# Softmax of the self-attention: two exponentials over 512 columns a slot, and row sums on VectorE

## What is computed

```python
tohd = lambda t: t.reshape(B, N, h, d).transpose(0, 2, 1, 3)
q, k, v = (make_fxp(tohd(q)), make_fxp(tohd(k)), make_fxp(tohd(v)))
dots = make_fxp(jnp.einsum('bhnd,bhmd->bhnm', q, k) * scale)
attn = make_fxp(jax.nn.softmax(dots, axis=-1))
attn = make_fxp(attn)
out = make_fxp(jnp.einsum('bhnm,bhmd->bhnd', attn, v))
```

## Time and profile before

| | us |
|---|---|
| median of 3 runs (lowest to highest) | 730.09 (729.47 to 730.7) |
| span of the profiled execution | 730.2 |
| TensorE matmul busy | 672.8 (92%) |
| VectorE busy | 550.0 (75%) |
| ScalarE busy | 413.7 (57%) |
| GpSimd busy | 272.6 (37%) |
| ScalarE, exponentials of self-attention (L819), x256 | 75.1 |
| ScalarE, their accumulator reads (L819), x256 | 49.9 |
| VectorE, reciprocals of self-attention (L1047), x32 | 6.5 |

### The profile page before, as it was taken

One profiled execution on the slowest core, in us unless ns is written; L12 is line 12 of the kernel. 1 busy time (PEld: TensorE's weight loads), 2 busy tenths in 40 slices (PEclk: granted clock), 3 DMA queues, 4 the chain that ended last, 5 costly groups with the idle time before them and its releaser, 6 DMA issues.

```text
span 730.2 us, 15676 instructions
## 1 busy us (share of the span) xinstructions
PE 672.8 (92%) x5186; PEld 551.7 (76%) x5186; DVE 550.0 (75%) x1142; ACT 413.7 (57%) x1443; POOL 272.6 (37%) x610
## 2 busy tenths in 40 slices
PE   5998879989998899878989999999999889999997
PEld 4777768777886788766777877787788777888986
DVE  5879887887888789757767776677667668787775
ACT  4677756767776777764455455445544563433432
POOL 1166754454445534535354344234333532010110
PEclk9999999999999999999999999999999999999999
DMA  9135100000000000050000000000000000000000
GB/s 312 49 111 150 60 30 1 1 1 1 0 0 0 0 0 0 0 153 1 1 2 16 1 1 1 14 0 0 0 0 0 0 1 1 2 30 0 29 29 29
DMA packets 17002, 18.75 MB, mean 26 GB/s; under 512 B 2851, under 2 KB 15427, under 8 KB 16963
## 3 DMA queue, kind: packets, MB, share of 16 engines
q1 hardware_dynamic: 15330, 15.11, 6.4%
q0 software_dynamic: 1632, 3.15, 1.5%
HBM read 16.16 MB, written 2.10 MB: 25 GB/s over the span
## 4 chain that ended last, share of the span: by engine, by line
PE 35%; POOL 7%; DVE 6%; ACT 3%; issue 3%; DVEq 0%; POOLq 0%; ACTq 0%
PE bank L405 9%; PE bank L407 8%; PE bank L406 8%; POOL p_f L363 6%; PE bank L583 3%; ACT e_sb L889 2%; PE bank L595 2%; PE bank L607 1%; DVE mx L1164 1%; PE bank L729 1%; PE bank L741 1%; DVE bn_st L966 1%; DVE oT_lo L1206 1%; POOL p_int L316 0%; DVE v_sb L1137 0%
## 5 line engine op out<-in xcount | busy, mean ns | idle before, releaser
L363 POOL TENSOR_SCALAR p_f<-e_sb,rsum 128x128 f32<-128x128 f32 x256 | 95.6, 398 | 156.7 <-DVE rsum L1199 156.7
L316 POOL TENSOR_SCALAR p_int<-e_sb,rsc 128x128 int16<-128x128 f32 x256 | 116.2, 475 | 6.3 <-issue 5.7
L889 ACT ACTIVATE e_sb<-bank,neg_max 128x128 f32<-128x128 f32 x256 | 90.1, 380 | 12.1 <-DVE neg_max L1168 11.9
L804 ACT ACTIVATE sgn<-bank 128x512 bf16<-128x512 f32 x96 | 57.2, 598 | 57.6 <-PE bank L407 57.6
L819 ACT ACTIVATE e_sb<-si 128x128 f32<-128x128 int16 x256 | 75.1, 303 | 0.0
L1021 DVE SCALAR_TENSOR_TENSOR ri<-sgn,bank 128x512 int16<-128x512 bf16 x96 | 62.5, 677 | 7.3 <-ACT sgn L804 6.5
L875 ACT COPY q_sb<-bank 128x512 f32<-128x512 f32 x32 | 18.8, 587 | 84.5 <-PE bank L407 84.5
L311 POOL TENSOR_TENSOR rsc<-rsum,growth 128x8 f32<-128x8 f32 x32 | 6.7, 209 | 156.0 <-DVE rsum L1047 156.0
L889 ACT ACTIVATION_READ_ACCUMULATOR e_sb<-bank,neg_max 128x1 f32 x256 | 55.9, 218 | 0.0
L405 PE MATMUL bank<-xnT_hi,wqkvT_lo 128*128 128x512 f32 x128 | 53.6, 419 | 2.2 <-DVE ri L1021 1.3
L1175 DVE COPY aT_sb<-bank 128x512 f32<-128x512 f32 x64 | 41.2, 685 | 12.7 <-PE bank L583 12.5
(11 more groups left out here) (162 smaller groups left out, 2039.5 us busy)
## 6 DMA issues: line engine op xcount, KB each, us to landing
x_sb<-in_x SPq DMA_DIRECT2D x4, 512.0 KB, 10.3
wqkv_raw<-in_L_attn_w_qkv SPq DMA_DIRECT2D x2, 1024.0 KB, 10.2
out<-x_sb SPq DMA_DIRECT2D x8, 256.0 KB, 2.2
wqkv_raw<-in_L_attn_w_qkv SPq DMA_DIRECT2D x2, 512.0 KB, 5.1
wp_raw<-in_L_attn_w_proj SPq DMA_DIRECT2D x1, 1024.0 KB, 12.3
raw_b<-in_L_xattn_Wq SPq DMA_DIRECT2D x2, 512.0 KB, 3.3
wq_hi<-in_L_xattn_Wq POOLq DMA_DIRECT2D x2, 512.0 KB, 4.1
wo_hi<-in_L_xattn_Wo POOLq DMA_DIRECT2D x2, 512.0 KB, 8.4
```

Of the source, the lines that this page charges most:

```text
L316: i = nc.gpsimd.tensor_scalar(p_int[:, t, :], e_sb[:, t, :], rsc[:, t:t + 1], -0.5, ALU.mult, ALU.add)
L363: i = nc.gpsimd.tensor_scalar(p_f[:, t, :], e_sb[:, t, :], rsum[:, t:t + 1], 0.0, ALU.mult, ALU.add)
L804: nc.scalar.activation(sgn[:, m % 2, :], proj_ps[m % 2][:, :], ACT.Sign).then_inc(a_sgn, 1)
L889: last = nc.scalar.activation(e_sb[:, t, :], s_ps[hh][:, (t % 4) * P:(t % 4 + 1) * P], ACT.Exp, bias=neg_max[:, t:t + 1], scale=DH ** -0.5 ...
```

## The change

An exponential with accumulator runs as two instructions on ScalarE, the activation and the read of its accumulator, and there were eight such pairs a slot, one for each score tile. The change makes one activation of each half of a slot, four tiles and 512 columns, without accumulator, each with its own count on `a_e`. VectorE forms the row sums: `a_recip` waits for each half in turn and sums it (four sums of 128 columns in one instruction), then waits on the new semaphore `a_sm` for its own two sums, and takes the reciprocal as before. Values are the same up to the order of addition in the sums. Nothing else is moved.

```diff
--- before.py
+++ after.py
@@ -210,6 +210,7 @@
 
     a_blk, a_sgn, a_ri, a_fx = sem("a_blk"), sem("a_sgn"), sem("a_ri"), sem("a_fx")
     a_S, a_ssgn, a_si, a_clip, a_e = (sem(n) for n in ("a_S", "a_ssgn", "a_si", "a_clip", "a_e"))
+    a_sm = sem("a_sm")
     a_rs, a_rsc, a_p, a_T, a_aT = (sem(n) for n in ("a_rs", "a_rsc", "a_p", "a_T", "a_aT"))
     a_av, a_osgn, a_oi, a_ohi, a_olo, a_pj = (sem(n) for n in ("a_av", "a_osgn", "a_oi", "a_ohi", "a_olo", "a_pj"))
     a_z, a_zn, a_zi, a_zf, a_x = (sem(n) for n in ("a_z", "a_zn", "a_zi", "a_zf", "a_x"))
@@ -814,11 +815,8 @@
                     wait(act, a_p, n)
                     wait(act, a_rs, n)
                 wait(act, a_clip, 2 * n + 1 + i)
-                for j in range(4):
-                    t = 4 * i + j
-                    last = nc.scalar.activation(e_sb[:, t, :], si[:, i, j * P:(j + 1) * P], ACT.Exp,
-                                                scale=1.0 / FIX, accum_out=sums[:, t:t + 1])
-                last.then_inc(a_e, 1)
+                nc.scalar.activation(e_sb[:, GB * i:GB * i + GB, :].rearrange("p a t -> p (a t)"), si[:, i, :], ACT.Exp,
+                                     scale=1.0 / FIX).then_inc(a_e, 1)
 
             def a_out_sign(n):
                 wait(act, a_av, n + 1)
@@ -1042,7 +1040,10 @@
                 V.tensor_tensor(oT_lo[:, :], oi[:, :], oT_hi[:, :].bitcast(F32), ALU.subtract).then_inc(a_olo, 1)
 
             def a_recip(n):
-                wait(dve, a_e, 2 * n + 2)
+                for i in range(2):
+                    wait(dve, a_e, 2 * n + 1 + i)
+                    V.reduce_sum(sums[:, GB * i:GB * i + GB], e_sb[:, GB * i:GB * i + GB, :], AX).then_inc(a_sm, 1)
+                wait(dve, a_sm, 2 * n + 2)
                 wait(dve, a_p, n)
                 V.reciprocal(rsum[:, :], sums[:, :]).then_inc(a_rs, 1)
 
```

## The result

The changed kernel takes 745.35 us (median of 4 runs, 742.97 to 748.27), beside 730.05 us (729.47 to 730.70) for the kernel before on the same chip. The ratio is 1.021, with an interval of 1.0184 to 1.0237. In a second session it was 744.08 (743.55 to 746.35) against 730.26, 1.020 [1.0186, 1.0214]. So it is slower, as forecast (738.3), but the loss is 15.3 us where 8.25 were summed, and 745.35 lies above the top of the range, 742.5.

A forecast was written before the change was run, and what follows sets the result against it. Slots 4 to 7 were taken as chain-bound, slots 1 to 3 as without slack in VectorE's queue. Groups' 3.85 + 0.9 + 2.2 and last reciprocal's 1.3 gave +8.25 on 730.2: 738.3 us, range 732.5 to 742.5.

The forecast's parts named there:

- slot 1: Steady group: VectorE reaches the reciprocal late, so bank reading and TensorE's next projection come 0.3 us later.
- slot 2: Steady group: VectorE free early, reciprocal 0.3 earlier; TensorE gains 0.05 us, VectorE enters slot 3 some 0.3 ahead.
- slot 3: Steady group: reciprocal 207.96 instead of 206.94, bank reading 0.64 later, nothing before TensorE to hide it: +0.6 us.
- slot 6: Steady group: VectorE 0.4 us ahead by then, so the reciprocal comes 0.2 us earlier again.
- group 0, slot 1: Reciprocal had no idle time before it: +1.3 us, straight into TensorE's wait for the bank.
- group 0, slots 4 to 7: Slot 4 +1.3 us into the wait for `p_int`, slot 5 +0.75 (late F), slot 6 +0.1, slot 7 +0.7.
- last reciprocal: At 330.03 us, reached late by VectorE, with GpSimd's products behind it on the last chain: +1.3 us.
- The rule of F and E: VectorE reaches reciprocal at F, exponentials start at E: reciprocal from later of F, E + 2.46 to later of F, E + 0.64, plus 1.31.
- The third rival: Clock falls behind grown `p_int` waits, group 0 slot 4 and stage end: up to 1.7 us each, 741.7; chance 0.08.
- The second rival: Bank edge in slots 1 and 3 is coincidence, only waits for `p_int` move: 2.4 us less, 736; chance 0.14.
- The first rival: With sums near 415 ns, chain-bound slots give up to 0.5 to 1 us each: 728, down to 724; chance 0.09.
- The fourth: Gains of slots 0, 2, 5, 6 and losses of 1, 3, 4, 7 cancel, no change; chance 0.07.

The follow-up runs named there:

- the two filled kernels: Unused 512-column matmuls put into TensorE's waits of the changed kernel, 738.72 us, and the same matmuls put into the kernel before, 731.65 us.
- the filled kernel: The changed kernel, all slots new, with unused 512-column matmuls put ahead of TensorE's long waits: 738.72 us, 1.0102.
- the two with chosen slots: Changed kernel with old form in slots 1 and 3 of groups 1-3 and group 0's slot 1: 737.81 us; new form only where VectorE comes early: 727.02 us.
- the half-wide one: Kernel before, in chosen slots first four tiles in one 512-column exponential summed by VectorE, other four with accumulators: 724.35 us, 0.9911.
- the added sums: Kernel before with accumulators kept and two row sums, read by nobody, added on VectorE before each reciprocal: 774.68 us, 1.0599.
- the kernel with the new form in the early slots: Kernel before with the new form only in slots 2, 3 of group 0 and 0, 2, 5, 6 of groups 1 to 3: 727.02 us, 0.9944.
- filling the one slot: Kernel before with new form only in group 0's slot 1, six unused matmuls put into TensorE's grown wait: 731.58 us; unfilled 732.64 us.

## Why the prediction was right in its direction and short in its size

The steps can be held against TensorE's transposes, one per slot (intervals between their starts, after less before; steady group unless named):

| step | predicted, us | measured, us |
|---|---|---|
| slot 1 | +0.3 | +0.33 |
| slot 2 | -0.05 | -0.05 |
| slot 3 | +0.6 | +0.89 |
| slot 4 | +0.35 | +0.30 |
| slot 5 | -0.5 | -0.45 |
| slot 6 | -0.2 | +0.04 |
| slot 7 | +0.7 | +0.68 |
| slot 0 | -0.1 | -0.13 (into group 2) |
| group 0, slot 1 | +1.3 | +1.3, and 1.6 of lost clock behind it |
| group 0, slots 2 and 3 | -0.3 | -0.36 |
| group 0, slots 4 to 7 | +1.3, +0.75, +0.1, +0.7 | +1.31, +0.72, +0.09, +0.68 |
| last reciprocal | +1.3 | +2.05, of it the clock at 332 to 336 |

*The rule of F and E* held, and with it the costs of the pieces (675 ns a sum, two in a row 1.27 us). Slots 4 to 7 of group 0 came within 0.03 us each. In the last row both executions had a fall; between the two filled kernels, which have none there, the step is +1.0 (11.90 against 10.87).

*Two terms of the sum were mis-sized*, slots 3 and 6: together 0.5 us in each steady group, which measures +1.6 and not +1.1, some 1.5 us in the three groups. *Slot 3* was 0.3 us short. Here is VectorE in it, then TensorE's first projection behind it:

```profile
211.37 0.69 DVE L1069 SCALAR_TENSOR_TENSOR zi<-raw_b,near 128x512 int16<-128x512 f32 x1
211.98 1.27 DVE L1045 TENSOR_REDUCE sums<-e_sb 128x4 f32<-128x512 f32 x2
213.29 0.20 DVE L1048 RECIPROCAL rsum<-sums 128x8 f32<-128x8 f32 x1
213.41 0.65 DVE L1035 SCALAR_TENSOR_TENSOR oi<-o_sgn,bank 128x512 int16<-128x512 bf16 x1
...
215.31 1.27 DVE L1019 SCALAR_TENSOR_TENSOR ri<-sgn,bank 128x512 int16<-128x512 bf16 x2
```

```profile
216.04 0.50 PE L406 MATMUL bank<-xnT_hi,wqkvT_lo 128*128 128x512 f32 x1 [0.82 <-DVE ri L1019]
```

The order of VectorE's work is as foretold: no idle time before the sums, 2.02 us from the reciprocal to the bank reading instead of 2.38, and TensorE starts 0.06 us behind the reading's end. But the prediction let VectorE enter the slot 0.3 us ahead, from slot 2, and that lead is not there. In slot 2 VectorE, early by those 0.3 us, stands still again for another release:

```profile
204.80 0.69 DVE L1019 SCALAR_TENSOR_TENSOR ri<-sgn,bank 128x512 int16<-128x512 bf16 x1 [0.40 <-ACT sgn L805]
```

It waits 0.40 us for ScalarE's `sgn`, which waits for TensorE; a lead on one engine lasts only to its next wait for another. So the slot's loss was 0.89 in each steady group. The second rival, that this edge is soft, is out.

*Slot 6* was to gain 0.2 and gained nothing. Again VectorE's lead is gone before it reaches the sums. These are its scaling of q and its sums in the changed kernel; below them, from the profile of before, the scaling and the addition to `x_sb` that GpSimd makes at that time:

```profile
236.08 0.92 DVE L1023 TENSOR_SCALAR q_sb<-ri 128x512 f32<-128x512 int16 x1
...
238.31 1.27 DVE L1045 TENSOR_REDUCE sums<-e_sb 128x4 f32<-128x512 f32 x2
```

```profile
230.54 0.57 DVE L1025 TENSOR_SCALAR q_sb<-ri 128x512 f32<-128x512 int16 x1
```

```profile
229.55 1.28 POOL L325 TENSOR_TENSOR x_sb<-x_sb,raw_b 128x512 f32 x1
```

In the changed kernel GpSimd's addition starts at 235.44 and takes 1.28 us as well. Counted from the transposes of the slot, VectorE begins its bank readings 0.3 us earlier than before, so the scaling that follows lies deeper inside GpSimd's addition: 0.6 us of overlap and not 0.3. It takes 0.92 us and not 0.57 (0.41 in most other slots of the steady groups), and the lead is used up; the sums then start without idle time, 2.79 us behind the transposes, where VectorE had reached the reciprocal at 2.83 before. The 0.92 stands in slot 6 of groups 1 to 3 in all four kernels with wide exponentials and both sums in slots 5 and 6 (the changed, the filled and the two with chosen slots); in the half-wide one the scaling takes 0.57 as before, and its slot 6 gains 0.55. That the overlap with GpSimd is the cause is read from these rows, and no run moves GpSimd's addition to test it. The prediction knew the effect, at 2.03 us in group 0, and did not apply it here.

*Group 1* is not to be read slot by slot: the DMA that GpSimd waits for came in 3.6 us there instead of 4.8, and a fall of before's profile in it has no counterpart after. The DMAs of the start differ too between executions: in the profile of after TensorE's first projections start 0.8 us later than in that of before, ahead of anything that was changed.

*The step that failed is the clock.* The sum gave it nothing. The third rival named the mechanism (a grown wait of TensorE with the clock falling behind it), priced it at 3.4 us at most, in two places, and gave it 0.08; the range reached to 742.5, just over its 741.7. It is in the typical execution, and costs some 5 to 8 us: 5.7 and 6.7 by span times clock, 5.4 to 6.6 by the filled kernel against the two medians of the changed one, 8 by the loss of 15.3 less the 7.3 of the filled kernel. What it had wrong:

- the places. It looked only at waits for `p_int`. The dearest fall that the kernel before does not have (1.6 us) came behind the wait for the bank in group 0, slot 1, which was already priced at +1.3 as a plain shift. Of its two places, the end of the stage has a fall (332 to 336), but before has one there too; behind slot 4 of group 0 TensorE waits 3.20 us in the profile of after, the longest of these waits, and the clock stays at 1.00. In the profile above there was also a fall at the start of group 3: a wait of 2.02 us for `p_int`, then `aT_sb` times `v_sb` at 1.98 us where it is 1.09 at full clock, and that interval 1.35 us longer; the same wait of 2.02 us at 99.97 and 177.67 had none behind it:

```profile
253.97 0.62 PE L465 MATMUL bank<-ident_b,p_int 128*128 128x128 bf16 x8 [2.02 <-POOL p_int L317]
...
256.39 1.98 PE L476 MATMUL bank<-aT_sb,v_sb 128*64 128x128 f32 x16
```

- "behind such a wait TensorE has slack", the argument against it, holds in slots 4 to 7: in the second session's profile the clock falls behind slot 4 of group 0 (0.67 at 72 to 76), the next wait for `p_int` is 0.40 us and not 1.89, and the interval is 9.06 as without the fall. It does not hold in slots 0 to 3, where TensorE has no wait left to absorb a fall (+1.6 in group 0, slot 1, +1.35 in group 3, slot 0), nor in the last chain.
- it read a single execution of before. The falls are not at fixed places: the second session's profile of the changed kernel had them at 40 to 44, 72 to 76, 100 to 104 and 332 to 336 us. Between the profiles their number grows with the waits (two in the stage before, three and four after, ten between 36 and 368 us with the added sums).

With the sum of 8.25 and 6 us for the clock the forecast would have been 744.3, from the median. A smaller slip, which moved nothing: the sum was set on a span of 730.2 as if it equalled the median time, but a run's time is its span and some 1.8 us, and the profiled execution of before was at the long end of its runs (others have spans of 727.4 to 731.2).

*The first rival* (the chain counts, 724 to 728) would need cheap sums; with none at all the time is 719.3, below even its 724. *The fourth* (gains and losses cancel) fell with group 0 and slot 3.

Still open is what decides, in one execution, whether a fall follows a given wait; why the kernel with the new form in the early slots kept its clock near 1.0; and the gain from filling the one slot rests on intervals that touch.

## What to carry to other kernels

Before moving work from one engine to a less busy one, find for each slot the moment at which the receiver reaches the instruction that waits for that work. A lead that it gains in one slot is not to be carried into the next: here it was lost twice, at a wait for `sgn` and beside GpSimd's addition. Where the receiver arrives early, the move is a gain, and where it arrives late, the whole of the moved work is a loss, whatever its share of busy time; choose slot by slot, or move only as much as fits into the wait (here half a slot in some slots, 0.9911, where all of it in all slots gave 1.021).

When a wait of TensorE grows by a microsecond in many places, put a price on the clock as well: here it added some 6 us to some 8, and a first look at it is the mean granted clock of several executions, not the windows of one. Filling such waits with unused matmuls gave most of that back here, and nothing in the kernel before.

## What the runs showed of the hardware

- Behind a wait of TensorE of 2.37 us the next 4 us had a granted clock of 0.57 in one execution (three matmuls 1.44 us from start to start and not 0.80), and behind one of 2.40 us, at the same place in another execution of the same kernel, it stayed at 1.00. The mean clock over all went from 0.994 to 0.998 (before) to 0.984 to 0.991 (after) and 0.974 to 0.976 (accumulators and sums), as the waits shown for `p_int` and `ri` went from 24.0 to 32.6 and 51.7 us in one profile each. At one place, 4 of 5 profiles with a wait of 2.37 to 2.41 us have a fall behind it, and none of 8 with a wait of at most 1.08 us.
- Unused matmuls in that idle time brought the clock to 0.997 to 0.999 and made a kernel with more work 5.4 to 6.6 us faster; in the kernel before they changed nothing (1.0001, mean clock 0.994 to 1.0). One profile of each filled kernel still has a fall, behind or near waits that were not filled (0.69 at 68 to 72 us, 0.57 at 104 to 108).
- A row sum over 512 columns f32 takes 675 ns from SBUF, 677 from PSUM, and two in a row take 1.27 us.
- VectorE's scaling of 512 columns to `q_sb` takes 0.41 us in most slots of the steady groups, 0.57 and 0.92 us where it lies 0.3 and 0.6 us inside GpSimd's addition to `x_sb`.
